# Spline attention on one core: keys in 25 tiles of 128 instead of 28 tiles of 112 for turning and weighting

## What is computed

```python
sim = jnp.einsum('bhnd,bhdm->bhnm', q, k) / math.sqrt(dh)
xs = _safe(sim)                                   # clipped to -6..6
kan = base_w[0, 0] * jax.nn.silu(xs) + jnp.einsum('...k,k->...', b_splines(xs), coef)
attn = jax.nn.softmax(kan, axis=-1)
out = jnp.einsum('bhnm,bhmd->bhnd', attn, v)
```

## Time and profile before

| | us |
|---|---|
| median of 3 runs | 7482.52 (7480.34 to 7487.51) |
| span of the profiled execution, first to last instruction | 7470.2 |
| `kan_attention3`, from its first transfer to the end | 2050 to 7470 |
| one block in the steady part | 27.32 |
| TensorE clock granted, mean | 0.974 |

### The profile page before, as it was taken

The page is one execution under the profiler, slowest core; times in us unless marked ns, Lnnn a source line. Parts: engine busy times, 40 slices in busy tenths (PEclk is TensorE's granted clock), DMA queues, the critical chain, the costliest instruction groups (busy, mean ns, idle before and its releaser), DMA issues. The chain is left out here.

```text
span 7470.2 us, 142915 instructions
## 1 busy us (share of the span) xinstructions
PE 6708.3 (90%) x41336; PEld 4573.5 (61%) x41336; DVE 6259.6 (84%) x9621; ACT 5790.6 (78%) x9066; POOL 5398.4 (72%) x3374
## 2 busy tenths in 40 slices
PE   6877889999789999999999999999999999999998
PEld 4656547777546666666666666666666666666666
DVE  4333664444389999999999999999999999999998
ACT  5454113233189999999999999999999999999998
POOL 4333000000089999999999999999999999999997
PEclk8888999999889999999999999999999999999998
DMA  2000000000110000000000000000000000000000
GB/s 74 19 22 22 1 1 0 0 1 0 54 17 1 1 1 1 1 1 11 1 1 1 1 1 1 2 28 1 1 1 1 1 2 2 4 4 4 4 4 6
DMA packets 75948, 56.12 MB, mean 8 GB/s; under 512 B 50776, under 2 KB 73464, under 8 KB 75032
## 3 DMA queue, kind: packets, MB, share of 16 engines
q1 hardware_dynamic: 72512, 53.88, 2.6%
q10 hardware_dynamic: 3288, 0.33, 0.0%
HBM read 37.80 MB, written 16.37 MB: 7 GB/s over the span
## 5 line engine op out<-in xcount | busy, mean ns | idle before, releaser
L1532 POOL TENSOR_TENSOR a_s<-a_s,a_v 128x784 f32<-128x784 f32 x1568 | 2912.7, 1858 | 307.2 <-ACT a_s L1743 285.7
L1568 PE MATMUL a_right_sides<-a_s,diag_d 128*128 128x392 f32 x6272 | 2284.3, 507 | 8.3 <-POOL a_s L1532 1.0
L1568 PEld LDWEIGHTS a_right_sides<-a_s,diag_d 128*128 128x128 f32 x6272 | 1132.1, 190 | 1052.0 <-POOL a_s L1532 309.2
L1664 DVE SCALAR_TENSOR_TENSOR a_kan<-a_s,spline_c,a_kan 128x784 f32<-128x784 f32 x1568 | 1622.9, 1035 | 50.4
L1591 PEld LDWEIGHTS a_weighed<-a_V,a_probT 112*128 112x128 f32 x10976 | 1374.3, 193 | 162.2
L1525 POOL TENSOR_TENSOR a_inner<-a_inner,a_x 128x784 f32<-128x784 f32 x784 | 1458.5, 1860 | 0.0
L1591 PE MATMUL a_weighed<-a_V,a_probT 112*128 112x65 f32 x10976 | 1365.1, 270 | 0.0
L1743 ACT ACTIVATE a_s<-a_v 128x784 f32<-128x784 f32 x1568 | 1335.6, 852 | 4.7
L1734 ACT ACTIVATE a_v<-a_a 128x784 f32<-128x784 f32 x1568 | 1336.5, 853 | 0.3
L1580 PE MATMUL a_turned<-ident,a_prob 128*112 128x128 f32 x5488 | 856.4, 278 | 230.7 <-ACT a_probT L1750 229.1
L1635 DVE TENSOR_SCALAR a_x<-a_scores 128x392 f32<-128x392 f32 x1568 | 877.5, 560 | 20.2 <-PE a_scores L1555 20.2
(11 more groups left out here) (194 smaller groups left out, 6094.2 us busy)
## 6 DMA issues: line engine op xcount, KB each, us to landing
rows<-bias_rows_dram SPq DMA_DIRECT2D x112, 91.0 KB
X<-in_x_dram SPq DMA_DIRECT2D x4, 1568.0 KB, 13.8
a_q<-q_dram SPq DMA_DIRECT2D x392, 16.0 KB, 2.0
mask<-in_window_mask_dram SPq DMA_DIRECT2D x56, 98.0 KB
v_dram<-V SPq DMA_DIRECT2D x14, 227.5 KB, 2.3
a_V<-v_dram SPq DMA_DIRECT2D x4, 796.2 KB, 9.2
q_dram<-Q SPq DMA_DIRECT2D x14, 224.0 KB, 1.9
k_dram<-K SPq DMA_DIRECT2D x14, 224.0 KB, 1.9
```

The source lines that it names most:

```text
L1532: eng.tensor_tensor(s, s, v, ALU.mult).then_inc(cubed, 1)
L1568: mm = eng.matmul(up[:, j, 0:SUB], steps[i][:, :], cubes[g][:, SUB * j:SUB * (j + 1)], start=(i == 0), stop=(i == 1))
L1664: eng.scalar_tensor_tensor(F, banked((s1, s2)[j][g][:, :]), c[:, 3 + j:4 + j], F, ALU.mult, ALU.add).then_inc(left_added, 1)
```

## The change

The keys are cut into 25 tiles of 128 for turning and weighting: 24 at 128 * k and a last one at L - 128 = 3008, so that it overlaps tile 23 by 64 keys. Those 64 rows are zero in V, the column of ones too. Chunks are still of four tiles, 512 keys, so that there are six full ones and a seventh of one tile. In `project3` V has 128 partitions and 25 tiles; POOL sets the ones in two memsets and the zeros in a third, each waiting for the one before, and SP waits for all three. V's last chunk has one tile instead of four, for PE, DVE and SP. In `kan_attention3` `turn(6)`, `copies(6)` and `weigh(6)` handle one tile. `turn`'s `last` and `gate`'s counts of turned chunks follow from the new borders: `last` is now 0, 1, 1, 2, 3, 3, 3 for chunks 0 to 6, and was 0, 1, 1, 2, 2, 3, 3. The quarters, the lists of stages and their order stay.

```diff
--- before.py
+++ after.py
@@ -1272,6 +1272,19 @@
 BLOCKS3 = PAIRS3 * TILES3
 
 
+TAIL3 = L % P
+KEY_TILES3 = L // P + 1
+CHUNKS3 = -(-KEY_TILES3 // 4)
+
+
+def tiles3(ch):
+    return range(4 * ch, min(4 * ch + 4, KEY_TILES3))
+
+
+def first_key3(k):
+    return min(P * k, L - P)
+
+
 def pipeline_pairs(eng, stages):
 
 
@@ -1311,7 +1324,7 @@
         k.fold = keep("fold_heads", [P, QT3])
         k.q_dram = [dram(f"q3_dram{b}", (P, L)) for b in range(B)]
         k.k_dram = [dram(f"k3_dram{b}", (P, L)) for b in range(B)]
-        k.v_dram = [dram(f"v3_dram{b}", (TILE, TILES, 2 * V1)) for b in range(B)]
+        k.v_dram = [dram(f"v3_dram{b}", (P, KEY_TILES3, 2 * V1)) for b in range(B)]
         spline_constants3(nc, m, k)
         for b in range(B):
             project3(nc, m, b, k)
@@ -1351,7 +1364,7 @@
         sb = lambda name, shape: st.enter_context(nc.sbuf_tensor(f"{name}_{b}", shape, F32))
         xn = sb("xn3", [P, HALVES, L])
         Q, K = sb("Q3", [P, L]), sb("K3", [P, L])
-        V = sb("V3", [TILE, TILES, 2, V1])
+        V = sb("V3", [P, KEY_TILES3, 2, V1])
         pp = [st.enter_context(nc.psum_tensor(f"p3p{i}_{b}", [P, 512], F32)) for i in range(8)]
         sem = st.enter_context(signals(nc, f"p3_{b}"))
         normed, made, kept_a, kept_v, ones_set, stored = (sem(n) for n in ("normed", "made", "kept_a", "kept_v", "ones_set", "stored"))
@@ -1359,11 +1372,16 @@
         with nc.Block() as block:
             @block.gpsimd
             def _(pool):
-                pool.memset(V[:, :, :, VW:V1], 1.0).then_inc(ones_set, 1)
+                last = KEY_TILES3 - 1
+                pool.memset(V[:, 0:last, :, VW:V1], 1.0).then_inc(ones_set, 1)
+                pool.wait_ge(ones_set, 1)
+                pool.memset(V[P - TAIL3:P, last, :, VW:V1], 1.0).then_inc(ones_set, 1)
+                pool.wait_ge(ones_set, 2)
+                pool.memset(V[0:P - TAIL3, last, :, :], 0.0).then_inc(ones_set, 1)
 
             @block.sync
             def _(sp):
-                sp.wait_ge(ones_set, 1)
+                sp.wait_ge(ones_set, 3)
                 for k in range(CHUNKS):
                     cols = slice(CHUNK * k, CHUNK * (k + 1))
                     sp.wait_ge(kept_a, 2 * k + 1)
@@ -1371,7 +1389,8 @@
                     sp.wait_ge(kept_a, 2 * k + 2)
                     sp.dma_start(k3.k_dram[b][:, cols], K[:, cols]).then_inc(stored, 16)
                     sp.wait_ge(kept_v, k + 1)
-                    sp.dma_start(k3.v_dram[b][:, 4 * k:4 * k + 4, :], V[:, 4 * k:4 * k + 4, :, :].rearrange("p j h c -> p j (h c)")).then_inc(stored, 16)
+                    some = slice(tiles3(k).start, tiles3(k).stop)
+                    sp.dma_start(k3.v_dram[b][:, some, :], V[:, some, :, :].rearrange("p j h c -> p j (h c)")).then_inc(stored, 16)
                 sp.wait_ge(stored, 16 * 3 * CHUNKS)
 
             @block.vector
@@ -1381,8 +1400,9 @@
                     dve.tensor_scalar(xn[:, f, :], m.X[:, u, :], m.rstd[:, u:u + 1], m.nbias[:, u:u + 1], ALU.mult, ALU.add).then_inc(normed, 1)
                 for k in range(CHUNKS):
                     dve.wait_ge(made, 3 * k + 3)
-                    dve.tensor_copy(V[:, 4 * k:4 * k + 4, :, 0:VW],
-                                    pp[(3 * k + 2) % 8][0:TILE, :].rearrange("p (j h c) -> p j h c", j=4, h=2)).then_inc(kept_v, 1)
+                    low, n = (0, 4) if k < CHUNKS3 - 1 else (P - TAIL3, 1)
+                    dve.tensor_copy(V[low:P, 4 * k:4 * k + n, :, 0:VW],
+                                    pp[(3 * k + 2) % 8][low:P, 0:P * n].rearrange("p (j h c) -> p j h c", j=n, h=2)).then_inc(kept_v, 1)
                 dve.wait_ge(kept_v, CHUNKS)
 
             @block.scalar
@@ -1410,10 +1430,10 @@
                             mm = pe.matmul(bank[:, 0:CHUNK], m.WT[:, (W_Q3, W_K3)[j] + i, :], xn[:, i, CHUNK * k:CHUNK * (k + 1)],
                                            start=(i == 0), stop=(i == 1))
                     else:
-                        for q in range(4):
-                            at = TILE * (4 * k + q)
+                        for q, tile in enumerate(tiles3(k)):
+                            at = first_key3(tile)
                             for i in range(HALVES):
-                                mm = pe.matmul(bank[0:TILE, P * q:P * (q + 1)], xn[:, i, at:at + TILE], m.WT[:, W_V3 + i, :],
+                                mm = pe.matmul(bank[:, P * q:P * (q + 1)], xn[:, i, at:at + P], m.WT[:, W_V3 + i, :],
                                                start=(i == 0), stop=(i == 1))
                     mm.then_inc(made, 1)
 
@@ -1427,10 +1447,10 @@
         sb = lambda name, shape: st.enter_context(nc.sbuf_tensor(f"a3_{name}", shape, F32))
         ps = lambda name, shape: st.enter_context(nc.psum_tensor(f"a3_{name}", shape, F32))
         K = [sb(f"K{r}", [P, 4, SUB]) for r in range(2)]
-        V = [sb(f"V{r}", [TILE, TILES, V1]) for r in range(2)]
+        V = [sb(f"V{r}", [P, KEY_TILES3, V1]) for r in range(2)]
         q = [sb(f"q{r}", [P, QT3]) for r in range(2)]
         prob = [sb(f"prob{r}", [P, L]) for r in range(2)]
-        probT = [sb(f"probT{r}", [TILE, 4, P]) for r in range(2)]
+        probT = [sb(f"probT{r}", [P, 4, P]) for r in range(2)]
         x = [sb(f"x{g}", [P, QUART]) for g in range(4)]
         a = sb("a", [P, QUART])
         v1 = [sb(f"v1{g}", [P, QUART]) for g in range(2)]
@@ -1447,7 +1467,7 @@
         scp = ps("scores", [P, 2, 512])
         up = ps("right_sides", [P, 2, 512])
         fp = ps("kan", [P, 2, 512])
-        tp = ps("turned", [TILE, 4, P])
+        tp = ps("turned", [P, 4, P])
         op = ps("weighed", [P, V1])
         yp = up[:, :, SUB:SUB + QT3]
         folded = scp[:, 0, SUB:SUB + QT3]
@@ -1570,14 +1590,14 @@
                     return stage
 
                 def turn(ch):
-                    last = min(4 * TILE * (ch + 1) - 1, L - 1) // QUART
+                    last = min(4 * P * (ch + 1) - 1, L - 1) // QUART
 
                     def stage(eng, t, r, p):
                         eng.wait_ge(exp_done, 4 * t + last + 9)
                         eng.wait_ge(copied, 7 * t + ch + 1)
-                        for j in range(4):
-                            at = TILE * (4 * ch + j)
-                            mm = eng.transpose(tp[:, j, :], prob[r][:, at:at + TILE], m.ident[:, :])
+                        for j, k in enumerate(tiles3(ch)):
+                            at = first_key3(k)
+                            mm = eng.transpose(tp[:, j, :], prob[r][:, at:at + P], m.ident[:, :])
                         mm.then_inc(turned, 1)
                     return stage
 
@@ -1586,9 +1606,8 @@
                         if ch == 0:
                             eng.wait_ge(placed, 2 * t + 2)
                         eng.wait_ge(copied, 7 * t + ch + 2)
-                        for j in range(4):
-                            k = 4 * ch + j
-                            mm = eng.matmul(op[:, :], probT[(r + ch) % 2][:, j, :], V[p % 2][:, k, :], start=(k == 0), stop=(k == TILES - 1))
+                        for j, k in enumerate(tiles3(ch)):
+                            mm = eng.matmul(op[:, :], probT[(r + ch) % 2][:, j, :], V[p % 2][:, k, :], start=(k == 0), stop=(k == KEY_TILES3 - 1))
                         mm.then_inc(weighed, 1)
                     return stage
 
@@ -1624,7 +1643,7 @@
                 def gate(g):
                     def stage(eng, t, r, p):
                         eng.wait_ge(right_made, 4 * t + g + 5)
-                        eng.wait_ge(turned, 7 * t + min(2 * g + 2, 7))
+                        eng.wait_ge(turned, 7 * t + (2, 4, 5, 7)[g])
                         eng.scalar_tensor_tensor(banked(part(r, g)), banked(x[g][:, :]), 0.0, U, ALU.is_gt, ALU.mult).then_inc(right_gated, 1)
                     return stage
 
@@ -1747,7 +1766,8 @@
                     def stage(eng, t, r, p):
                         eng.wait_ge(turned, 7 * t + ch + 15)
                         eng.wait_ge(weighed, 7 * t + ch + 1)
-                        eng.copy(probT[(r + ch) % 2][:, :, :], tp[:, :, :]).then_inc(copied, 1)
+                        n = len(tiles3(ch))
+                        eng.copy(probT[(r + ch) % 2][:, 0:n, :], tp[:, 0:n, :]).then_inc(copied, 1)
                     return stage
 
                 def place(eng, t, r, p):
```

## The result

| | us |
|---|---|
| before, median of 4 runs | 7481.43 (7480.09 to 7487.51) |
| changed, median of 4 runs | 7818.72 (7809.01 to 7822.88) |
| ratio | 1.0449, 95% interval 1.0434 to 1.0463 |
| forecast | 7625, range 7585 to 7685 |
| span of the profiled execution before, changed | 7470.2, 7817.3 |

The change makes the kernel 4.5% slower. The way was forecast, the size was not: +337 us against +143.

A forecast was written before the change was run, and what follows sets the result against it. DVE was taken to bound the kernel. Stalls of 97 x 0.59 + 97 x 0.95 = 149 us, less 6 of small parts, gave +143 on the 7470.2 us span; with 12.3 to the median 7625 us, range 7585 to 7685.

The forecast's parts named there:

- DVE sets the pace: Steady part: DVE busy 27.00 of 27.32 us per block, so savings on PE and ACT cost at 0.
- turn(4) waits for exponent(3): PE's queue: one new wait per block delays scores(3) and right_side(1), for which DVE's clip(3,0) and gate(1) wait.
- The stall per block, 0.59 and 0.95 us: DVE standing at clip(3,0) and gate(1): 0.59 us per block in even pairs, 0.95 in odd ones.
- Odd pairs are later by 0.36 us: keep_o on the upper partitions makes exponent(3) start 3.21 us after tanh(0) instead of 2.85.
- The clock stays up: PE's granted clock stays 1.00 despite the new gap of 1.6 to 2.0 us per block.
- a rival: PE's clock falls in the new gap, 1.7 us per block if in every block, 7960 us; 4 in 100.
- The cover on ACT holds: ACT absorbs the late copies(5), reaching tanh(2) 0.15 to 0.2 us early; rival of its loss 7684 us, 10 in 100.
- The small parts, -6 us: Outside the steady part: project3 -3.4 us, V transfer +0.2, memsets 0, the end -3.1.
- The 12.3 us from span to median: Added to the forecast span of 7613 us, as the amount by which the median of the runs lies above it.
- PE would win 1.15 us in a block: Three of 28 transposes and weightings fewer; rival that this shortens the kernel, 7257 us, 3 in 100.

The follow-up runs named there:

- e1: Changed kernel with chunks of 4, 4, 4, 4, 2, 4, 3 tiles, so that turn(4) needs exponent(2) alone; 7464.25 us, ratio 0.9978.
- e2: Kernel before, with 28 tiles of 112, in which turn(4) waits for exponent(3) instead of exponent(2), nothing else; 7959.34 us, ratio 1.0638.
- e5: Changed kernel with turn(4) behind scores(3) in PE's list instead of ahead of it; 7478.18 us, ratio 0.9993.
- e7: Changed kernel with fold_heads, keep_o and project_out on partitions 0 to 63 in all pairs; 7761.79 us, ratio 1.0383.
- e4: Changed kernel with needless PE products of 384 and 256 columns ahead of turn(1) and turn(2), away from turn(4)'s gap; 7864.19 us, ratio 1.0515.
- e6: Changed kernel with the first two tiles of turn(4) transposed before the wait for exponent(3), the last two behind it; 7702.80 us, ratio 1.0303.
- e3: Changed kernel with two needless PE products ahead of turn(4), the wait for exponent(3) now behind that for `copied`; 7675.14 us, ratio 1.0254.

## Why the prediction was wrong, point by point

- **DVE sets the pace, work saved on PE and ACT gives nothing in the steady part: right.** e1 saves all of it, and its blocks last 27.31 us instead of 27.32. The saving had a second side that was weighed only as a cover: e2, without it, is 140 us slower than the changed kernel.
- **turn(4) waits for exponent(3), clip(3,0) and gate(1) stand behind it: right**, by place, by order and by count (193 of the forecast 194). e1 and e5 take it away in two different ways and both end within 0.3% of the kernel before.
- **The stall per block, 0.59 and 0.95 us: a little small.** Undisturbed blocks show 0.74 and 1.10. The missing 0.15 us are hand-overs. The earlier trace rows gave 0.05 from the exponent to turn(4) and 0.03 from PE to DVE, but the first was read at the end of the kernel, outside the loop. In the loop they are 0.13, then 0.07 to clip(3,0) and 0.14 to gate(1): turn(4) and gate(1) have a second wait behind the one that ends last, and so a register instruction between (gate's, L1646, at 5166.38). Over 194 blocks these 0.15 us are 29 us. 128 columns of weights for a transpose cost nothing to be seen: turn(4) to scores(3) still took 0.58.
- **Odd pairs are later by 0.36 us: right** (28.42 against 28.06), and e7 ties it to the partitions. PE's gap too came out as forecast, 1.6 us in even pairs and up to 2.0 in odd ones. The odd pairs, with the longer gap, were hit by the low clock more often: 54 of 84 blocks looked at, against 36 of 84; in e7, with all pairs alike, 18 or 19 of 42 in each.
- **The clock stays up: this is the step that failed.** The forecast's sum has no term for the clock. 103 of 191 blocks had a low stretch, at 1.66 us each. The prediction had the mechanism as a rival, with its price per block, 1.7 us, measured as 1.66. It gave it 4 in 100, by the reasoning that one gap in 28 us beside 24 us of work is harmless, and it priced it only for all blocks or none (7960). More work beside the gap did not help (e4), and one gap of 1.6 to 2.0 us was enough in about half of the blocks. 171 us, the greater part of the miss: without it the time would have been 7648, inside the range.
- **The cover on ACT holds: right in the changed kernel** (tanh(0) and tanh(2) come straight after their clips, with ACT idle ahead), and as thin as stated: in e2, without the smaller copies(6), it is gone.
- **The small parts, -6 us: as large as forecast in sum, partly by luck.** From project3 to the first clip 96.1 us instead of 100.8, 4.7 less (3.2 forecast); behind the last row maximum 34.1 instead of 35.7, 1.6 less (3.1). Both terms are off by about half, one each way, and one execution can't tell them from noise: the part ahead of project3, whose code is the same, took 5.3 us longer. The three memsets cost nothing to be seen.
- **The 12.3 us from span to median were read wrongly.** In every run listed the time is only 1.7 to 2.0 us above the span; the other 10 us or so are those by which the profiled execution was faster than the median. As a step from that span to a median the sum holds.
- The Trainium skill's rule (Trainium Kernel Development and Optimization, Best Practices), to tile to 128 partitions always, was set aside as one that moves nothing here. That was right for the tiles by themselves: in e1, where nothing else is lost, they are worth 0.2%. That PE would win 1.15 us in a block and the kernel nothing is what e1's blocks of 27.31 us show.

## What to carry to other kernels

When a tile size changes, list again which producer each chunk's last column reaches, and look not at the wait that moves but at what stands behind it in that engine's queue: 25 tiles with the border kept (e1) or the entry moved by one place (e5) cost nothing. In a loop, put the wait that ends last behind the other ones: a second wait behind it cost 0.08 us in each block here. On an engine with a throttled clock a new gap has two prices, the stall and what runs slower behind it, and the second can be as large as the first. Price such a gap as happening in some of the blocks, not in all or none, and don't take one kernel's clean clock as proof that its gaps are harmless: at another length of the block the same gap can be hit.

## What the runs showed of the hardware

- A gap of 1.6 to 2.0 us on PE, with PE busy for 86% of the time, was followed by a stretch at the lower clock in 102 of 191 blocks. With the longest gap there cut to 1.16 us (e6) it was 57, with the gap filled with needless products none (e3). In the kernel before, whose gaps are up to 1.1 us, and in e1, with up to 1.33, one block in 191 had a low stretch, the last.
- Length alone does not decide. Behind the gap ahead of scores(1), of much the same length in both kernels, the clock fell once in the changed kernel and 50 times in e3. Between two blocks with the same gap the place of its end decides, against the evenly spaced moments at which the level can change: 0 of 78 in one part, 86 of 87 in the other.
- With needless work in the gap the kernel is faster (7675 against 7819 us).
- A hand-over from ACT to PE took 0.05 us where the second wait has a constant, 0.13 in the loop (20 and 176 of 196 rounds). In e6, where the wait for exponent(3) is the last thing before the transposes, it was 0.05 in all 196.
- An ACT copy of 512 columns takes 0.58 us on average in the changed kernel, one of 128 columns 0.25: by these two, some 0.14 us of it do not depend on the columns, an estimate.
